# Expert tiles from rolling queues, their weighted outputs added to the output by accumulating indirect transfers

## The reference, cut to what matters

```python
probs = jax.nn.softmax(xf @ gate_w + gate_b, axis=-1)      # 8 experts
top2_vals, top2_idx = jax.lax.top_k(probs, 2)
cw = jnp.zeros((N, Ee)).at[jnp.arange(N)[:, None], top2_idx].add(top2_vals)
def step(acc, params):
    w1, bb1, w2, bb2, we = params
    h = jax.nn.gelu(xf @ w1 + bb1, approximate=False)
    y = h @ w2 + bb2
    return (acc + we[:, None] * y, None)
...
t = t + _L1_ffn_ref(_ln_t(t), L1_ffn_gate_w, L1_ffn_gate_b, L1_ffn_W1, L1_ffn_b1, L1_ffn_W2, L1_ffn_b2)
```

## Time and profile before

| what | value |
|---|---|
| runs, median of 3 | 2999.1 us (2977.64 to 3004.55) |
| profiled execution | 2989.77 us, of it the span 2988.0 us |
| busy: PE, DVE, ACT, POOL | 84%, 67%, 63%, 56% of the span |
| granted TensorE clock, mean | 0.932 of full speed |
| moved by DMA | 422.65 MB |

### The profile page before, as it was taken

The page is one execution under the profiler, slowest core; times in us unless marked ns, Lnnn a source line. Parts: engine busy times, 40 slices in busy tenths (PEclk is TensorE's granted clock), DMA queues, the critical chain, the costliest instruction groups (busy, mean ns, idle before and its releaser), DMA issues. The chain is left out here.

```text
span 2988.0 us, 75732 instructions
## 1 busy us (share of the span) xinstructions
PE 2511.1 (84%) x27338; PEld 1770.3 (59%) x27338; DVE 1996.7 (67%) x5193; ACT 1872.4 (63%) x3478; POOL 1670.3 (56%) x1626
## 2 busy tenths in 40 slices
PE   6888898888998889889989898888988787766673
PEld 3465555656666666666666666665666565544452
DVE  3678877887666666776766687777866676543223
ACT  3666666667667677677777677777766565443231
POOL 1224445554333444565555566777637888877765
PEclk9999999999999999899999899999999798977897
DMA  6233344335445554153443444554433333347674
GB/s 216 103 115 124 132 166 158 128 129 201 135 135 177 171 182 166 59 155 101 123 123 112 119 135 117 149 148 131 137 105 111 113 107 98 100 129 256 193 240 158
DMA packets 255504, 422.65 MB, mean 141 GB/s; under 512 B 42044, under 2 KB 141512, under 8 KB 252688
## 3 DMA queue, kind: packets, MB, share of 16 engines
q1 hardware_dynamic: 209632, 322.59, 33.5%
q0 software_dynamic: 35456, 72.95, 8.1%
q10 hardware_dynamic: 10048, 22.28, 2.4%
HBM read 205.05 MB, written 231.63 MB: 146 GB/s over the span
## 5 line engine op out<-in xcount | busy, mean ns | idle before, releaser
L1308 POOL DMA_INDIRECT x_sorted<-xn_c,place_i x512 | 537.1, 1049 | 333.5 <-PE bank_s L780 127.4
L1298 POOL TENSOR_TENSOR s_sb_a<-s_sb_a,mx_a 128x512 f32<-128x512 f32 x256 | 268.0, 1047 | 675.9 <-DVE mx_a L1703 675.0
L1329 POOL DMA_INDIRECT yg<-y_sorted,place_i x320 | 317.7, 993 | 187.9 <-PE bank_to L863 84.1
L1695 DVE TENSOR_TENSOR s_sb_a<-bank_s,bias_a 128x512 f32<-128x512 f32 x256 | 176.5, 690 | 327.1 <-PE bank_s L780 242.7
L1320 POOL DMA_INDIRECT y_tokens<-yo,back_to x276 | 284.9, 1032 | 93.8 <-issue 73.9
L909 PE MATMUL bank_m<-xe,wk_e 128*128 128x512 f32 x552 | 279.5, 632 | 47.6 <-ACT hid L1176 27.9
L917 PE MATMUL bank_m<-wk_e,hid 128*128 128x128 f32 x2208 | 288.0, 294 | 1.2 <-ACT hid L1176 1.2
L917 PEld LDWEIGHTS bank_m<-wk_e,hid 128*128 128x128 f32 x2208 | 282.5, 211 | 2.6 <-issue 1.9
L1298 POOL TENSOR_TENSOR s_sb_b<-s_sb_b,mx_b 128x512 f32<-128x512 f32 x256 | 269.9, 1054 | 0.3
L1142 ACT ACTIVATE p_sb_a<-s_sb_a 128x512 f32<-128x512 f32 x256 | 160.8, 628 | 161.0 <-POOL s_sb_a L1298 160.5
L841 PE MATMUL bank_to<-k_consts,p_sb_b 128*128 128x128 f32 x1024 | 178.5, 300 | 91.3 <-ACT pt_sb_a L1137 66.0
(11 more groups left out here) (233 smaller groups left out, 5947.0 us busy)
## 6 DMA issues: line engine op xcount, KB each, us to landing
y_sorted<-t_back SPq DMA_DIRECT2D x192, 512.0 KB, 5.2
wk_e<-in_w_experts_dram SPq DMA_DIRECT2D x134, 321.0 KB
xs<-x_sorted SPq DMA_DIRECT2D x134, 258.0 KB
y_sorted<-yo SPq DMA_DIRECT2D x101, 256.0 KB
t_kept<-t SPq DMA_DIRECT2D x64, 256.0 KB
xin<-in_x_dram SPq DMA_DIRECT2D x128, 112.0 KB
x_res<-in_x_dram SPq DMA_DIRECT2D x256, 56.0 KB
t_back<-t_kept SPq DMA_DIRECT2D x23, 512.0 KB
```

The source lines that it names most:

```text
L1298: pool.tensor_tensor(s[:, :, :], s[:, :, :], m[:, :, None].to_broadcast(shape), ALU.subtract).then_inc(s_sub[w], 1)
L1308: pool.indirect_dma_start(out=x_sorted[group_of[d] % XSIDES].ap(), out_offset=bass.IndirectOffsetOnAxis(ap=place_i[:, d % KEPT, TILES * ch ...
L1329: pool.indirect_dma_start(out=yg[:, c % 2, n, :], out_offset=None, in_=y_sorted[side].ap(), in_offset=bass.IndirectOffsetOnAxis(ap=place_i ...
L1695: tt(s_sb[0][:, :, :].rearrange("p (r h) n -> p r (h n)", h=2), scores, bias_a[:, kind, :, :].rearrange("p (r h) n -> p r (h n)", h=2), AL ...
```

## The change

The groups go. Each expert keeps one queue of rows in a single `x_sorted`, which rolls on from image to image, and with each image the four next **full** tiles of 512 rows are taken, from whichever experts have them (1 tile for image 1, 4 for images 2 to 30, the remaining 18 with image 31): 135 tiles. `tile_table` runs for each image from image 1 on, with a running start for each expert. A pass has two slots instead of three, with PE's parts in steps 1, 2, 3 and 6, 7, 0; the tail has 11 pairs (22 tiles). A scattered row carries its token number (`HOME`) and its gate weight (`SHARE`). `slots_back` adds the bias in PSUM and then multiplies by the weight into `yo`. SP stores the image's own rows (`spill`) straight to the output, and POOL's `add_back` adds each tile's rows to the output by four indirect transfers with `compute_op=ALU.add`. Two experts can add to the same token, so a tile's first transfer waits until all four of the tile before have landed (`landed(pool, q)`). `y_sorted`, its zeros, `y_tokens`, `t2_kept`, `gather`, `sum_experts`, `store_image` and `bring_back` are gone. The output tensor has 512 more rows, for padding rows of the last tiles.

```diff
-GROUPS = (7, 7, 6, 5, 4, 3)
...
+BATCH, FIRST_BATCH = TOP * TOKENS // SLOTS, 1
...
-SLOTS_PER_PASS = 3
...
+SLOTS_PER_PASS = 2
+HOME, SHARE, ROW_W = D, D + 1, D + 2
+BACK_AT = (((4, 0), (4, 1), (4, 2), (4, 3), (5, 1), (5, 2), (6, 1), (6, 2)),
+           ((9, 0), (9, 1), (9, 2), (9, 3), (10, 1), (10, 2), (10, 3), (11, 1)))
...
+def tiles_of(m):
+
+    return 1 if m == FIRST_BATCH else BATCH if m < IMAGES - 1 else LAST_TILES
...
+            last = i == PASSES - 1 and n == SLOTS_PER_PASS - 1
+            if i >= pairs[u].batch + (5 if n == 0 else 4) and not last:
                 here[n] = u
...
-            into = slot(i, 0) if t == 1 else slot(i, 1) if t == 3 else slot(i, 2) if t == 6 else None
-            mid = slot(i, 0) if t == 2 else slot(i, 1) if t == 4 else slot(i, 2) if t == 7 else None
-            back = slot(i, 0) if t == 3 else slot(i, 1) if t == 5 else slot(i - 1, 2) if t == 0 else None
+            into = slot(i, 0) if t == 1 else slot(i, 1) if t == 6 else None
+            mid = slot(i, 0) if t == 2 else slot(i, 1) if t == 7 else None
+            back = slot(i, 0) if t == 3 else slot(i - 1, 1) if t == 0 else None
...
+        def landed(eng, done):
+
+            if done > 0:
+                k = (done - 1) % YO
+                eng.wait_ge(y_back[k], 16 * SUB * len(range(k, done, YO)))
...
             def spill(c, h):
                 need_half(sp, ln_c, c, h, LN_STEPS, 1)
...
+                        sp.dma_start(out_rolled[c, r, c0:c1, tiles, :],
+                                     t2[SIDE * r + p0:SIDE * r + p1, tiles, :]).then_inc(t2_out[h], 16)
...
+            def add_back(u, k):
+
+                _, q, _ = pairs[u].members[k // SUB]
+                j = k % SUB
+                if j == 0:
+                    for h in range(2):
+                        pool.wait_ge(t2_out[h], 16 * IO_DMAS * (pairs[u].batch + 1))
...
+                    landed(pool, q)
+                    pool.wait_ge(ids_kept, q + 1)
                     pool.wait_ge(yo_ready, q + 1)
-                j = k % MOVES
-                pool.indirect_dma_start(out=y_tokens[pairs[u].group].ap(),
+                pool.indirect_dma_start(out=out,
                                         out_offset=bass.IndirectOffsetOnAxis(ap=back_to[:, q % IDS, j:j + 1], axis=0),
-                                        in_=yo[:, q % YO, j, :], in_offset=None).then_inc(y_back[q % YO], 16)
...
+                                        in_=yo[:, q % YO, j, :], in_offset=None, compute_op=ALU.add).then_inc(y_back[q % YO], 16)
...
+            def second_shares(d, h):
 
                 dve.wait_ge(scattered[h], 16 * (TILES * d + 4))
-                homes_of(d, 1, slice(4 * h, 4 * h + 4))
+                shares(d, 1, slice(4 * h, 4 * h + 4))
...
+            def slots_back(pair, banks):
+
+                for m, q, _ in pair.members:
+                    dve.wait_ge(y_done, q + 1)
+                    y = banks[:, m, :].rearrange("p (j d) -> p j d", j=SUB)
+                    bias = wk_b[buffer_of(q)[0]][:, None, B2_AT:B2_AT + D]
+                    tt(y, y, bias.to_broadcast([P, SUB, D]), ALU.add).then_inc(y_biased, 1)
+                for m, q, _ in pair.members:
+                    landed(dve, q - YO + 1)
+                    dve.wait_ge(y_biased, q + 1)
+                    y = banks[:, m, :].rearrange("p (j d) -> p j d", j=SUB)
+                    share = xs_b[buffer_of(q)[0]][:, :, SHARE:SHARE + 1]
+                    tt(yo[:, q % YO, :, :], y, share.to_broadcast([P, SUB, D]), ALU.mult).then_inc(yo_ready, 1)
```

More of the change, by code:

```diff
@@ new lines, in hybrid_kernel @@
+        tiles_before = sb("tiles_before", [1, E + 1])
+        first_row = sb("first_row", [1, E + 1])
+        begun = sb("begun", [1, LAST_TILES, E + 1])
+        begun_rows = sb("begun_rows", [1, LAST_TILES, E + 1])
+        begun_count = sb("begun_count", [1, LAST_TILES])
+        row_of = sb("row_of", [1, LAST_TILES])
+        taken_before = sb("taken_before", [1, E + 1])
+        taken = sb("taken", [1, E])
+        table = [sb(f"table{n}", [1, 2 * LAST_TILES + E], I32) for n in range(TABLES)]
@@ L906, in hidden @@
                         pe.wait_ge(gelu_ready, CH * q + ch - 1)
-                    for h in range(PART):
-                        own = slice(SLOTS * h, SLOTS * h + SLOTS)
-                        last = mm(banks[:, ch, own], w[:, h, P * ch:P * ch + P], xe[:, m, own], start=True, stop=True)
-                    last.then_inc(z_ready, 1)
+                    mm(banks[:, ch, :], w[:, P * ch:P * ch + P], xe[:, m, :], start=True, stop=True).then_inc(z_ready, 1)
             def expert_out(q, m, end, banks):
@@ L1173, in gelu @@
                     act.wait_ge(z_ready, CH * q + ch + 1)
-                    for h in range(PART):
-                        own = slice(SLOTS * h, SLOTS * h + SLOTS)
-                        last = func(hid[:, CH * m + ch, own], banks[:, ch, own], ACT.Gelu,
-                                    bias=w[:, h, B1_AT + ch:B1_AT + ch + 1])
-                    last.then_inc(gelu_ready, 1)
+                    func(hid[:, CH * m + ch, :], banks[:, ch, :], ACT.Gelu,
+                         bias=w[:, B1_AT + ch:B1_AT + ch + 1]).then_inc(gelu_ready, 1)
             act.preload_act_table_set(EXP_LN_SET)
@@ L1267, in step @@
                     layer_rstd(ln_b, b, 1, mv_b, rs_b)
-                if t in (1, 3) and into is not None:
+                if t == 1 and into is not None:
                     slots_copy(into, bank_m)
@@ L1335, in step @@
                 n, nb = TILES * i + t, TILES * i + t - LAG
-                now, before = sums[i] if i >= 0 else [], sums[i - 1] if i > 0 else []
-                def share(lo, hi, k):
-                    return range(lo + (hi - lo) * k // 4, lo + (hi - lo) * (k + 1) // 4)
                 def moves(k):
@@ L1353, in moves @@
                         scatter(d - 1, 12 + k)
-                    first = (0, 4, 8, 12, 16) if len(now) == 1 else (0, 6, 12, 16, 16)
-                    if now and 1 <= t <= 4:
-                        for row in share(first[t - 1], first[t], k):
-                            gather(now[0], row)
-                    first = (0, 6, 8, 10, 12)
-                    if len(now) > 1 and t >= 4:
-                        for row in share(first[t - 4], first[t - 3], k):
-                            gather(now[1], row)
-                    if len(before) > 1 and t == 0:
-                        for row in share(12, TOP * TILES, k):
-                            gather(before[1], row)
                 if tiled(n):
@@ L1385, in _ @@
             for u in tail:
[L1386 to L1387 removed]
+                for k in range(SUB * len(pairs[u].members)):
+                    add_back(u, k)
         @block.vector
@@ L1724, in step @@
                 into, mid, back = stage(i, t)
-                now = sums[i] if i >= 0 else []
-                late = sums[i - 1][1:] if i > 0 else []
                 if tiled(n):
@@ L1745, in step @@
                 if back is not None:
-                    for m, q, _ in back.members:
-                        slots_back(q, m, bank_m)
+                    slots_back(back, bank_m)
                 if t == 0:
@@ L1768, in step @@
                         layer_norm_stats(ln_c, c, 1, t2, st_c, mv_c)
-                    for s in late:
-                        sum_experts(s, (0, 1, 2))
                 if t == 2:
@@ L1799, in step @@
                         layer_norm_apply(ln_b, b, 0, t1[b % 2], mv_b, rs_b, xn_b)
-                    if now:
-                        sum_experts(now[0], (0,))
-                if t >= 6 and on(d) and d >= first_late:
-                    second_homes(d, 7 - t)
+                if t >= 6 and on(d):
+                    second_shares(d, 7 - t)
                 if t == 6:
@@ L1813, in step @@
                         unit_vectors(f, 0)
-                    if now:
-                        sum_experts(now[0], (1, 2))
                 if t == 7:
```

533 lines of the change are left out of this document (167 added, 366 removed).

## The result

The changed kernel takes 3122.3 us (median, 3114.1 to 3125.42), against 2993.92 of the kernel before in the same comparisons: a ratio of 1.0429, 95% interval 1.0375 to 1.0484. The forecast was 2877, its range ended at 2995. The profiled span is 3123.6, against 2988.0 before and 2875 forecast, 249 too little.

The account below looks back on a forecast made before the run. PE bounds six-tile passes, POOL's transfer queue passes 29, 30 and the tail. 481.5 to pass 7, 1980 for passes 7 to 30, 183, 142 for transfers, 82 for waits, 4.5 and 2: span 2875, time 2877; range 2740 to 2995.

Parts of the forecast that it names:

- base of the passes: Passes 7 to 30: a pass with four tiles was taken at 80 us, from passes 10 and 17.
- doubled move: Step 3: DVE moves each tile by two operations instead of one; +0.5 us a pass.
- three additions to a pass: Passes 7 to 30: DVE's second move, tile table and POOL's additions raise a pass from 80 to 82.5 us.
- The tile table: Step 4 of every pass: fifteen DVE operations, 3.5 us with two small writes, mostly in idle time; +0.5 us.
- POOL's steps 5 and 6: Two additions on top of four scatters in each step, 2.5 us a step, almost all fitting; +1.5 us a pass.
- sign of being wrong: POOL's queue: the prediction would be wrong if the additions took POOL over 1.2 us.
- rival with a double issue: POOL's queue: issuing an addition costs 0.96 us more, in the tail and in steps 5 and 6; 3061, chance 0.05.
- landing: A tile's first transfer waits for the tile before: landing 4.5 us, hidden in passes, 3.4 each for 24 tiles at the end.
- cover by PE and the loads: Tail: PE's tiles take at most 5.7 us against POOL's 8.5, and six buffers load 50 us ahead.
- opening run backwards: Passes 31 to 34: priced from passes 2, 1 and 0 (160.7 together), +5 for tiles and 17 for pass 34; 183.
- The middle runs like six tiles: Passes 7 to 30: DVE's and POOL's parts in steps 3 to 6 become the chain; 86 a pass, 2961, chance 0.17.
- late landing: Tail and passes: additions land later than 4.5 us; over 3029 from a landing of 7.7, 3198 at 10; chance 0.13.

Follow-up runs that it names:

- unread matmuls: Changed kernel plus three matmuls of 512 columns that nobody reads, in step 4 only: 3018.89 us, ratio 1.0086; with six more in step 6, 3026.96 us.
- spread run: Changed kernel with the additions only in steps 1 to 4, four a step, and four yo buffers instead of three: 3061.25 us, ratio 1.0246.
- first run: Changed kernel with transfers that overwrite the output rows instead of adding (the sum is left out): 3047.44 us, ratio 1.0203.
- two targets: Changed kernel with odd tiles adding into a second tensor, so a tile waits for the one before the last; merging left out: 3062.9 us, ratio 1.024.

## Why the prediction was wrong

**The step that failed** is the base of the passes: "Two passes of the trace have four tiles: 80.50 (pass 10) and 79.50 (pass 17); I take 80." Both have their pairs in steps 3 to 5 and 6 to 0, and in both steps 0 to 2 hold no tile, since the pass before has none in 6 to 0. The change puts the pairs into 1 to 3 and 6 to 0, pass after pass. For these places the kernel before takes 83.4, without any of the change's additions; and the places of passes 10 and 17, taken pass after pass, cost 75.6. So 80 was the price of neither. The trace of the kernel before had a row for the price of the place, step 4 of pass 16, whose only tile stood in steps 1 to 3 (the third line is its passes 7 to 30):

```profile
1214.60 0.22 PE L825 MATMUL bank_to<-chosen,earlier 128*128 128x72 bf16 x1 [2.53 <-DVE ot_b L1719]
1213.52:1225.98 12.46, 10.52 (x91) 5.43 (x92) 8.89 (x38) 6.66 (x10) 3.02 (x3) 0.73 0.02 6
...
472.00:2456.90 1984.90, 1760.03 (x20115) 1263.61 (x20114) 1433.40 (x3826) 1388.18 (x2534) 1112.81 (x1084) 0.95 0.43 134
```

It is step 4 of the changed kernel almost to the digit: 12.46 against 12.49, 91 matmuls at 0.73, behind a wait of 2.53 for the same operation, though DVE there has one move for one tile. The clock stood in every row that I read, and I took it for a mean of PE's speed, not for a price of PE's waits. The base missed 3.4 of the 6.2 us a pass. The unread matmuls show that the clock behind the wait in step 4 is worth 4.7 a pass in the changed kernel; this overlaps with the base and with the doubled move below, so it is not a further term.

**The three additions to a pass** (2.5 forecast, 5.3 found).
- The doubled move, +0.5: leaving one out gave 3.6. I had asked how long DVE was idle (0.74), not who waits behind it: the moves stand in step 3, ahead of the `ot_b` that PE waits for, and there is less time at half clock with one move than with two. The link between the move and the clock is argued from the order of the queue; the wait itself changed by 0.3.
- The tile table, +0.5: by the trace it is hidden; no run left it out. DVE's timeline of pass 18 has its first and last operation, 2.6 us from end to end, and then the next scores, for which DVE is still idle for 3.08, as in the earlier trace rows:

```profile
1513.30 0.34 DVE L1458 SCALAR_TENSOR_TENSOR rows_left<-place,start_row 1x8 f32<-1x8 f32 x1
...
1515.73 0.15 DVE L1487 TENSOR_TENSOR start_row<-start_row,taken 1x8 f32<-1x8 f32 x1
...
1518.97 0.69 DVE L1510 TENSOR_TENSOR s_sb_a<-bank_s,bias_a 128x512 f32<-128x512 f32 x1 [3.08 <-PE bank_s L637]
```

- POOL's steps 5 and 6, +1.5: the place was right. POOL's timeline shows step 6's subtraction without idle time before it, where the earlier trace rows have 2.30 a step later:

```profile
1530.82 0.96 POOL L1142 DMA_INDIRECT x_sorted<-xn_c,place_i  x1 [0.31 <-issue]
1531.80 1.05 POOL L1135 TENSOR_TENSOR s_sb_a<-s_sb_a,mx_a 128x512 f32<-128x512 f32 x1
1532.81 1.04 POOL L1135 TENSOR_TENSOR s_sb_b<-s_sb_b,mx_b 128x512 f32<-128x512 f32 x1
```

The spread run takes 2.9 a pass off. These gains overlap, so they don't sum to the 5.3.

**Issue and landing.** The issue of 0.96, from plain transfers, is 1.58, above the 1.2 that the prediction had named as a sign of being wrong. The rival with a double issue had a chance of 0.05 because all plain forms cost the same; that says nothing of a form that no row shows. The landing came out near the forecast. In the tail

```profile
3096.66 1.56 POOL L1159 DMA_INDIRECT out_dram<-yo,back_to  x1 [0.30 <-issue]
3100.79 1.56 POOL L1159 DMA_INDIRECT out_dram<-yo,back_to  x1 [2.57 <-issue]
3102.65 1.56 POOL L1159 DMA_INDIRECT out_dram<-yo,back_to  x1 [0.30 <-issue]
```

4.13 lie between a tile's last issue and the next tile's first (forecast 4.7), 1.86 between issues (1.27). A tile takes 3 x 1.86 + 4.13 = 9.7 instead of 8.5: 22 x 1.2 = 26 of the tail's 37; the rest is mostly one wait of POOL for DVE's `yo`, 12.7 near its start, where the cover by PE and the loads that the forecast counted on was missing. That 4.13 came near 4.7 was partly luck: the forecast went by plain landings of 4.20 and 4.87, but with plain transfers the same gap is only 3.1 in the tail (2922.52 to 2925.61 in the first run), and the adding makes it 1.0 longer. In the passes the wait is hidden, as forecast.

**Passes 31 to 34** I priced by the opening run backwards, 183, and put only 24 transfers behind them. The window above shows POOL busy for 194.81 of 275.7; with 0.30 between its 131 transfers it is taken for 234. So its queue goes on setting the pace there, as the trace suggests and no run proves: plain transfers bring the stage to 256, two targets to 265, and the rest of the 55 stays open. Nor is the 7 us before pass 7 explained (in the other runs of the changed kernel pass 7 begins between 480.3 and 493.4, in no clear order; 1 of the 7 is the forecast's own sum, since 3 a tile on top of 66.3 makes 69.3 + 72.3 for passes 5 and 6, not 68.5 + 72), or what the 8 us at half clock that stay in a pass still cost.

**The rivals.** "The middle runs like six tiles" named the right stage and nearly the size (86, found 88.7), with the queues of DVE and POOL as its cause; the runs put PE's clock between them and the time. The late landing, my slower case, did not come. That a pass of four tiles can be as dear as one of six, because the missing pair leaves a gap in PE's work, was not among the rivals.
